# A flag from three VectorE reductions and one transpose in place of 36 matmuls, and a new order at both ends of the kernel

## What is computed

```python
xn = _layernorm(x, axis=-1)                       # x: (16, 512, 256), fp32
# attention: 16 heads of 16, causal, then the output projection
scores = einsum('bhsd,bhtd->bhst', q, k); scores = where(mask, -inf, scores)
attn = softmax(scores / sqrt(D)); s = einsum('bse,fe->bsf', attn @ v, Wo)
# gated feed-forward: integer weights -127..127 (HIDDEN 768), scaled by 1/127
h = silu(xn @ wg.T) * (xn @ wu.T); g = silu(h @ wd.T)
x = x + s * g
```

## Time and profile before

| | us |
|---|---|
| median of 3 runs | 959.0 (958.51 to 959.18) |
| the profiled execution | 958.51 |
| its span, first to last instruction | 956.8 |

### The profile page before, as it was taken

One profiled execution on the slowest core, in us unless ns is written; L12 is line 12 of the kernel. 1 busy time (PEld: TensorE's weight loads), 2 busy tenths in 40 slices (PEclk: granted clock), 3 DMA queues, 4 the chain that ended last, 5 costly groups with the idle time before them and its releaser, 6 DMA issues.

```text
span 956.8 us, 22743 instructions
## 1 busy us (share of the span) xinstructions
PE 926.0 (97%) x9065; PEld 686.7 (72%) x9065; DVE 701.0 (73%) x950; ACT 584.7 (61%) x796; POOL 495.3 (52%) x672
## 2 busy tenths in 40 slices
...
GB/s 277 156 65 131 76 146 173 125 157 116 168 148 113 172 126 156 130 144 157 117 175 100 197 131 124 171 126 151 122 168 144 116 175 126 155 130 144 110 93 89
DMA packets 85467, 133.97 MB, mean 140 GB/s; under 512 B 13680, under 2 KB 35952, under 8 KB 85360
## 3 DMA queue, kind: packets, MB, share of 16 engines
...
...
## 4 chain that ended last, share of the span: by engine, by line
PE 86%; issue 4%; ACT 3%; POOL 2%; DVE 2%; DMA 2%; SPq 0%; ACTq 0%; POOLq 0%; DVEq 0%
PE bank L194 45%; PE values L529 13%; PE bank L434 12%; PE bank L496 9%; PE bank L447 5%; POOL o_compact L570 2%; ACT probs L504 2%; DMA o_reciprocals<-scratch_r 1%; ACT o_hi L577 1%; DVE gated L379 1%; PE bank L465 1%; POOL probs L511 1%; DVE row_max L459 0%; PE bank L672 0%; DMA scratch_r<-sum_reciprocals 0%
## 5 line engine op out<-in xcount | busy, mean ns | idle before, releaser
L459 DVE TENSOR_REDUCE row_max<-bank 128x2 f32<-128x768 f32 (+3 forms) x352 | 384.9, 1124 | 69.1 <-PE bank L447 65.2
L504 ACT ACTIVATE probs<-bank 128x1024 f32<-128x1024 f32 x320 | 320.3, 1024 | 124.9 <-PE bank L496 123.2
L511 POOL TENSOR_SCALAR_AFFINE_SELECT probs<-probs 128x256 f32<-128x256 f32 (+1 forms) x448 | 195.5, 454 | 276.8 <-ACT probs L504 274.5
L529 PE MATMUL values<-probs,v 128*17 128x512 f32 (+3 forms) x2048 | 166.2, 436 | 3.1 <-POOL probs L511 3.0
L393 POOL TENSOR_TENSOR h_lo<-gated,h_hi 128x512 fp32r<-128x512 f32 x96 | 125.1, 1303 | 70.2 <-ACT h_hi L390 67.9
L434 PE MATMUL bank<-k_stack,q_stack 64*128 64x128 f32 (+3 forms) x1024 | 156.9, 366 | 2.5 <-DVE row_max L459 1.4
L496 PE MATMUL bank<-q_stack,k_stack 64*128 64x512 f32 (+3 forms) x1024 | 142.0, 350 | 1.2 <-DVE row_max L459 0.7
L434 PEld LDWEIGHTS bank<-k_stack,q_stack 64*128 64x128 f32 x1024 | 84.2, 185 | 69.5 <-issue 30.4
L496 PEld LDWEIGHTS bank<-q_stack,k_stack 64*128 64x128 f32 x1024 | 82.8, 186 | 39.2 <-issue 17.1
L366 DVE SCALAR_TENSOR_TENSOR gated<-gated,bank 128x512 f32<-128x512 f32 x96 | 65.9, 686 | 58.3 <-ACT gated L363 58.3
L194 PE MATMUL bank<-xt_hi,wg_hi 128*128 128x256 f32 x384 | 99.2, 292 | 2.3 <-DVE gated L379 2.3
...
## 6 DMA issues: line engine op xcount, KB each, us to landing
...
```

The costliest lines, as they stand in the source:

```text
L459: signal(e.tensor_reduce(rows, scores, axis=AX.X, op=ALU.max), "d_sm")
L504: signal(e.activation(PR[:, (SCORES * beta + k) % SLOTS, :, :], both(banks), ACT.Exp, scale=SCALE_S), "d_ex")
L511: last = e.affine_select(out=diag, in_=diag, compare_op=ALU.is_ge, fill=0.0, base=0, pattern=[[0, many], [1, P]], channel_multiplier=-1)
L529: last = nc.tensor.matmul(PVB[32 * c:32 * c + VW, j * P:S], V[par][:, j, 4 * g + c, :], PR[:, (SCORES * beta + 5 * g + kind) % SLOTS, pari ...
```

## The change

Units `gm` are gone, with their matmuls, their three small reductions and the rows `f_gm` and `d_gm` of the counters. The flag is now made in `fl` alone. Index 0, on DVE: three maxima of absolute values straight over the low weights in SBUF (each 128x1536), and one over the three results. Index 1: PE transposes the 128 values into the bank `values`, DVE takes their maximum and writes the flag. The DMA through `LOWROW` is gone. HEAD and TAIL are written in a new order, with other banks; PERIOD is as it was. But for `gm`, the old and the new tables hold the same units.

```diff
-            if en == "dve" and k == 0:
-                after(e, "d_gm", 0, 2)
+            if en == "dve" and k == 0:
+                e.wait_ge(c_wl, len(W))
+                for i, w in enumerate("gud"):
+                    e.tensor_reduce(LOW[:, i:i + 1], W[w][1][:].rearrange("p t n -> p (t n)"), axis=AX.X, op=ALU.max,
+                                    apply_absolute_value=True).then_inc(s_flag, 1)
+                e.wait_ge(s_flag, 3)
                 e.tensor_reduce(LOW[:, 3:4], LOW[:, 0:3], axis=AX.X, op=ALU.max).then_inc(s_flag, 1)
-            elif en == "sp" and k == 0:
-                e.wait_ge(s_flag, 1)
-                e.dma_start(LOWROW, LOW[:, 3:4]).then_inc(s_lowrow, 16)
             elif en == "dve":
-                e.wait_ge(s_lowrow, 16)
-                e.tensor_reduce(LOW1[:], LOWROW, axis=AX.X, op=ALU.max).then_inc(s_flag, 1)
-                e.wait_ge(s_flag, 2)
+                e.wait_ge(s_flag, 5)
+                e.tensor_reduce(LOW1[:], PVB[0:1, 0:P], axis=AX.X, op=ALU.max).then_inc(s_flag, 1)
+                e.wait_ge(s_flag, 6)
                 e.tensor_scalar(FLAG[:], LOW1[:], 0.0, None, ALU.is_le).then_inc(s_flag, 1)
+            elif en == "pe" and k == 1:
+                e.wait_ge(s_flag, 4)
+                e.transpose(PVB[0:1, 0:P], LOW[:, 3:4], IDF[:]).then_inc(s_flag, 1)
...
-            e.wait_ge(s_flag, 3)
+            e.wait_ge(s_flag, 7)
             exact = e.value_load(FLAG[0:1, 0:1], min_val=0, max_val=1)
...
-    mk 0 10 01, wt 0 5, gm 0 1 2, hs 0 0, wt 0 6, ls 0 3, v 0 0 5, hs 0 1, rw 0 0, sm 0 11 34, mt 0 0 0, gg 0 3 6,
+    sm 0 10 34, mk 0 10 34, sm 0 11 56, fl 0 0, ls 0 3, rw 0 0, mt 0 0 2, gu 0 2 3, sm 0 12 01, mk 0 11 56, gg 0 3 4, mk 0 12 01,
```

More of the change, by code:

```diff
@@ new lines @@
+    gg 0 4 2, st 0 0 56, st 0 1 34, st 0 2 01, fl 0 1, if 0 0, st 0 3 56, sm 0 16 34, mk 0 16 34, gu 0 3 2, sm 0 17 01,
+    st 0 4 34, mk 0 17 01, pv 0 0, st 0 5 56, sm 0 18 01, mk 0 18 01, st 0 6 34, pv 0 1, lb 1 0, sm 0 19 56, la 2 0,
+    st 0 7 12, mk 0 19 56, dn 0 0 0, gg 0 5 3, gu 0 4 2, st 0 8 56, sm 0 20 01, sm 0 21 34, mk 0 20 01, mk 0 21 34, pv 0 2,
+    lx 1 0, lm 2 0, gu 0 5 2, lt 2 0, hs 0 3, pv 0 3, hs 0 4, pv 0 4, mt 0 1 1, qk 1 0 4, st 0 9 01, ls 1 0, qk 1 1 5,
+    gg 1 0 2, gu 1 0 0, hs 0 5, gg 1 1 1, v 1 0 5, st 0 10 01, st 0 11 23, qk 1 2 6, st 0 12 01, sm 1 0 23, ls 1 1,
@@ new lines @@
+    mk 1 13 34, sm 1 14 12, mk 1 14 12, pv 0 10, sm 1 15 56, st 1 0 34, pv 0 11, mk 1 15 56, st 1 1 12, sm 1 16 34,
+    mk 1 16 34, gg 1 4 0, sm 1 17 56, st 1 2 23, od 0 1, gu 1 3 1, os 0 0, gg 1 5 0, st 1 3 23, gu 1 4 4, mk 1 17 56,
+    sm 1 18 01, mk 1 18 01, sm 1 19 23, mk 1 19 23, dn 1 0 4, gu 1 5 0, lx 2 0, or 0 1, pv 1 0, st 1 4 45, st 1 5 23,
+    sm 1 20 01, zr 0 0, ob 0 1, pv 1 1, mk 1 20 01, st 1 6 56, qk 2 0 4, st 1 7 56, sm 1 21 01, mk 1 21 01, ls 2 0, hs 1 3,
+    on 0 1, qk 2 1 3, gg 2 0 5, ls 2 1, mt 1 1 4, pv 1 2, v 2 0 0, st 1 8 23, pv 1 3, st 1 9 56, os 0 1, gu 2 0 4, qk 2 2 3,
@@ new lines @@
+    qk 2 3 2, st 1 10 01, sm 2 0 56, st 1 11 34, ls 2 2, mk 2 0 56, pv 1 4, ls 2 3, pv 1 5, od 1 0, st 1 12 56, sm 2 1 23,
+    mk 2 1 23, st 1 13 01, sm 2 2 45, mk 2 2 45, hs 1 4, st 1 14 23, sm 2 3 01, mk 2 3 01, pv 1 6, sm 2 4 56, hs 1 5,
+    mk 2 4 56, sm 2 5 34, st 1 15 12, mk 2 5 34, pv 1 7, pv 1 8, sm 2 6 01, sm 2 7 56, mk 2 6 01, st 1 16 23, mk 2 7 56,
+    or 1 0, op 0 0 4, dn 1 1 1, gg 2 1 2, op 0 1 5, hs 2 0, sm 2 8 34, mk 2 8 34, sm 2 9 01, mk 2 9 01, st 1 17 56, pv 1 9,
+    sm 2 10 23, mk 2 10 23, st 1 18 45, xr 1 0, st 1 19 01, gu 2 1 6, mt 2 0 4, sm 2 11 23, mk 2 11 23, sm 2 12 56,
@@ L84 @@
+    mk 2 12 56, hs 2 1, gg 2 2 1, sm 2 13 23, mk 2 13 23, v 2 1 4, sm 2 14 01, mk 2 14 01, sm 2 15 56, mk 2 15 56, st 2 0 23,
+    pv 1 10""")
 PERIOD = table("""
```

75 lines of the change are left out of this document (21 added, 54 removed).

## The result

| | before | after |
|---|---|---|
| median | 959.09 us (957.36 to 960.26) | 966.53 us (963.75 to 968.83) |
| ratio | 1 | 1.0072, 95% interval 1.0057 to 1.0086 |
| the profiled execution | 958.51 | 964.97 |
| its span | 956.8 | 963.3 |

The changed kernel is slower by 7.4 us; the prediction had 961.2, with 964.5 as the top of its range. The medians of the table are of six executions each. All executions of the changed kernel on record are 23, from 963.75 to 968.83 us, with a median of 965.56. That is 6.5 us more than before, and the two profiled executions differ by 6.5 us as well. So 6.5 is the better figure for the loss, and what follows is measured against it.

What follows compares the result with a forecast made beforehand. PE was taken to bound the kernel nearly everywhere, with PE and DVE tied in the head. From the 959.0 us median, +2.8 behind the branch, -0.75 in the tail and 0.1 for `lx` gave 961.2 us, range 956.0 to 964.5.

Steps and rivals of the forecast that it cites:

- DVE as the bound of the head: Head up to the flag: DVE needs 35.9 us of work from 17.70 on, so PE's 4.0 us gain turns into waits.
- work moved behind the branch: Behind the branch: 4.05 us of PE work moved there, 1.04 us moved ahead, so PE has 3.0 us more to do.
- the `lx` step: Behind the branch: entry 1's input split follows the last `gu` closely; 0 to 1 us in the range, 0.1 in the forecast.
- rival 3: Around the branch: PE's clock falls in the new idle stretch and products behind start slow, 1.3 us, giving 962.5; chance 0.18.
- the term of +2.8: At the branch: PE resumes 0.2 us earlier with 3.0 us more to do; the difference travels unchanged through the 13 periods.
- The flag and the branch: End of the head: flag at 53.9 us, PE resumes 0.6 to 0.9 us later, at 54.7 us.
- Rival 1: Head: DVE is not the bound, PE's gain comes through; 958.5 us, or 954.3 with DVE out of the way; chance 0.17.
- The tail: Last entry's chain: ACT's copy moves up by 1.0 us, the broadcast by 0.6 to 0.9; taken as -0.75 us.

Runs made afterwards that it cites:

- clock_held: The changed kernel plus 41 matmuls of zeros, which nobody reads, where PE stood idle ahead of the branch: 962.82 us.
- clock_held_cheap: The changed kernel with those 41 matmuls of zeros and each of the three maxima over 16 elements instead of 1536: 961.78 us.
- after_old_tail: The changed kernel with only the TAIL table put back to the old order: 966.75 us.
- cheap_maxima: The changed kernel with each of the three maxima over 16 elements instead of 1536, the rest of the test left out: 964.10 us.
- tail_alone: The kernel before with only the new TAIL table: 957.48 us.

## Where the prediction was right and where it failed

**Right.** The price of the maxima (1.75 us each), DVE as the bound of the head (36.26 us busy, 35.9 predicted), the direction, that work moved behind the branch is lost time, the `lx` step as a small stall (0.45 us ahead of `qk 1 0`), and that the loss travels through the periods. That waits hide a slow clock ahead of the branch is borne out too (55.50 against 55.80 us).

The account at `pv 1 10`, where the changed kernel is 6.64 us behind, has three terms: 0.57 (PE goes on later at the branch), 4.56 (the stretch behind it at the full clock) and 1.51 (the clock in that stretch). The prediction had -0.2, 3.0 and 0.

**The first step that failed: the clock was left out of the sum.** The prediction counted 9 us of waits ahead of the branch, in pieces of 1 to 2 us, and said that the products behind it would start slow. It then made this rival 3, with a chance of 0.18 and a price of 1.3 us, and put nothing into the sum. Behind the branch it cost 1.5 us in the trace, and holding the clock gives 2.7 us by the medians. The only row that it was priced by came behind a wait of 3.30 us. The changed kernel shows 0.60 behind waits of which none was longer than 1.7 us; in the 25 us ahead of 55.50 PE was idle for 5.0 us, not 9. The Trainium skill ("TensorE: Matmul & The Clock Gate", A second HAM failure mode) tells of such a case, a clock that swings because PE idles a little between groups of matmuls; the trace agrees.

**The second: the term of +2.8 was too small.** It was 3.0 for the work behind the branch less 0.2 at the branch, with the rest priced at 0 to 1 us and counted as 0.1. Measured without the clock it is 4.56 + 0.57 = 5.1 us. Of the 1.56 beyond the 3.0, 0.8 are waits, 0.45 of them the `lx` step. The other 0.8 are busy time of PE, and what makes it is not told apart; the same 1.56 are there in `clock_held` and in `clock_held_cheap`.

**The flag and the branch.** 53.9 us were predicted for the flag and 54.44 measured, 54.16 in `after_old_tail` with no cast beside `wu_lo`. So the cast is at most 0.3 of it. In `after_old_tail` DVE is busy 35.7 of the 36.5 us up to the flag, no more than predicted; its gaps come to 0.75 us, where 0.2 or 0.3 were allowed. PE went on 1.06 us behind the flag, not 0.6 to 0.9. Together 0.8 us. The prediction also read PE's waits for row maxima before as 1.0 us in two; with the 0.72 us of the earlier trace rows they are 1.7 in three.

**Rival 1.** At half the price of the maxima or less it had 958.5 us; `cheap_maxima` takes 964.1. Its 954.3 us, were DVE out of the way, no run tests: in `clock_held_cheap` (961.8 us) DVE is still busy 9.86 of the 10 us from 30 to 40 with row maxima. The new order has waits of its own there: `sm 0 2` needs the bank of `gu 0 1`, 1.69 us, which DVE reads only behind two row maxima.

**The tail: right sign, half of the mechanism.** 0.75 us were to come from ACT's copy, earlier by 1.0. Counted from the last period, as the prediction asked, the copy comes 0.74 us sooner in `tail_alone`, and that brings 0.53 at the start of `o_lo`. The other 1.0 us is `o_lo` itself. Its 1.73 us stood in the earlier trace rows, beside 0.69 for the same instruction elsewhere, and were taken as a fixed length. That the changed kernel gains from the new tail is not shown.

Put in the place of the sum: 959.0 + 2.8 as predicted, 0.8 for flag and branch, 1.6 for what the stretch behind the branch takes beyond 3.0 and 1.5 for the clock, nothing for the tail, are 965.7 us, against 965.6 over all 23 executions. That it fits so well is in part luck, as the tail is open and traces of the same periods differ by 3.5 us.
